# Time mixing reads the previous row from the PSUM bank of the transposed rows

## What is computed

```python
x = x + attention(layernorm(x), Wq, bq, Wk, bk, Wv, bv, Wo, bo)   # softmax(q k^T / 16), causal
h = layernorm(x)
h_prev = rows of h moved down by one, zero in front of each batch
xr = mu_r * h + (1 - mu_r) * h_prev
xk = mu_k * h + (1 - mu_k) * h_prev
x = x + sigmoid(xr @ W_r.T) * (square(relu(xk @ W_k.T)) @ W_v.T)
```

## Time and profile before

| | |
|---|---|
| median of three runs | 363.28 us (363.27 to 363.58) |
| the profiled execution | 363.31 us, span 361.2 us |
| busy, share of the span | PE 98%, DVE 70%, ACT 66%, POOL 58% |
| DVE idle before its maximum (L667), until ACT kept the scores | 47.4 us, 37 times |
| POOL idle before a low part of the weights (L365), until the high part | 37.5 us, 19 times |
| HBM traffic | 10.66 MB, mean 30 GB/s |

### The profile page before, as it was taken

How to read it: one execution, slowest core, us unless ns; L and a number is a source line. 1 busy time by engine, 2 the same in 40 slices (tenths; PEclk the granted TensorE clock), 3 DMA queues, 4 the chain that set the end, 5 groups by cost and what they waited for, 6 DMA issues and landing times.

```text
span 361.2 us, 6799 instructions
## 1 busy us (share of the span) xinstructions
PE 352.3 (98%) x2469; PEld 323.9 (90%) x2469; DVE 253.9 (70%) x571; ACT 239.3 (66%) x468; POOL 208.8 (58%) x246
## 2 busy tenths in 40 slices
PE   8999999999999999999999999999999999999995
PEld 6888888989899898899998989989999999989885
DVE  3696888698946786954568786787767558673645
ACT  2446534988758557696655679577368877789572
POOL 3013230568767753489643257687155768699781
PEclk9999999999999999999999999999999999999999
DMA  7700000000012003003000000120000000000001
GB/s 209 227 2 1 2 0 3 0 3 1 2 48 70 1 2 116 3 0 117 1 3 0 2 0 3 32 86 1 3 29 31 1 2 2 30 31 0 31 29 60
DMA packets 11906, 10.66 MB, mean 30 GB/s; under 512 B 1889, under 2 KB 11874, under 8 KB 11874
## 3 DMA queue, kind: packets, MB, share of 16 engines
q1 hardware_dynamic: 10512, 10.23, 8.7%
q10 hardware_dynamic: 1362, 0.01, 0.2%
HBM read 6.04 MB, written 4.19 MB: 28 GB/s over the span
## 4 chain that ended last, share of the span: by engine, by line
PE 79%; DVE 7%; POOL 6%; ACT 4%; issue 3%; ACTq 0%; DVEq 0%
PE W L801 16%; PE W L798 16%; PE W L802 16%; PE O L971 7%; PE O L973 7%; PE O L972 7%; PE W L834 3%; POOL kT_hi L365 3%; DVE mix L714 2%; POOL mix_lo L370 1%; PE O L996 1%; DVE st L679 1%; ACT mix L472 1%; ACT st L453 1%; DVE h_row L700 1%
## 5 line engine op out<-in xcount | busy, mean ns | idle before, releaser
L365 POOL TENSOR_TENSOR p_lo<-st,p_hi 128x512 fp32r<-128x512 f32 (+1 forms) x71 | 80.9, 1156 | 38.6 <-ACT p_hi L417 37.5
L667 DVE TENSOR_TENSOR peak<-peak,W 128x512 f32<-128x512 f32 (+3 forms) x70 | 42.2, 603 | 47.7 <-ACT st L417 47.4
L417 ACT ACTIVATE st<-W 128x512 f32<-128x512 f32 (+1 forms) x79 | 42.5, 537 | 41.5 <-PE W L802 41.4
L971 PE MATMUL O<-v_hi,p_hi 128*128 128x258 f32 x241 | 69.0, 287 | 0.2 <-DVE x_in L689 0.2
L973 PE MATMUL O<-v_hi,p_lo 128*128 128x258 f32 x241 | 68.0, 282 | 0.0
L972 PE MATMUL O<-v_lo,p_hi 128*128 128x256 f32 x241 | 67.7, 281 | 0.0
L801 PE MATMUL W<-xT_lo,kT_hi 128*128 128x512 f32 (+2 forms) x188 | 65.9, 350 | 0.0
L798 PE MATMUL W<-xT_hi,kT_hi 128*128 128x512 f32 (+2 forms) x188 | 64.3, 342 | 0.0
L802 PE MATMUL W<-xT_hi,kT_lo 128*128 128x512 f32 (+2 forms) x188 | 63.3, 337 | 0.0
L453 ACT ACTIVATE st<-st 128x512 f32<-128x512 f32 (+1 forms) x79 | 44.7, 566 | 8.7 <-DVE st L679 8.6
L370 POOL TENSOR_TENSOR mix_lo<-mix,mix_hi 128x512 fp32r<-128x512 f32 (+2 forms) x36 | 40.4, 1149 | 17.5 <-ACT mix_hi L417 17.5
(11 more groups left out here) (144 smaller groups left out, 825.7 us busy)
## 6 DMA issues: line engine op xcount, KB each, us to landing
out_dram<-gate SPq DMA_DIRECT2D x15, 256.0 KB, 2.2
x_in<-in_L_attn_y_all_dram SPq DMA_DIRECT2D x7, 512.0 KB, 4.4
x_in<-in_L_attn_y_all_dram SPq DMA_DIRECT2D x2, 256.0 KB, 5.1
h_row<-in_L_attn_Wk_dram SPq DMA_DIRECT2D x1, 256.0 KB, 3.6
h_row<-in_L_attn_Wq_dram SPq DMA_DIRECT2D x1, 256.0 KB, 4.5
st<-in_L_attn_Wv_dram SPq DMA_DIRECT2D x1, 256.0 KB, 5.5
st<-in_L_attn_Wo_dram SPq DMA_DIRECT2D x1, 256.0 KB, 5.8
mix<-in_L_ffn_W_k_dram SPq DMA_DIRECT2D x1, 256.0 KB, 6.7
```

Source lines behind the costliest of these rows:

```text
L365: g.tensor_tensor(lo[:, r], score_tile(u), hi[:, r].bitcast(f32), ALU.subtract).then_inc(p_split, 1)
L417: a.activation(dst, src, ACT.Copy, **kw).then_inc(done, 1)
L667: v.tensor_tensor(peak[:, J % 2, r], peak[:, J % 2, r], scores, ALU.max).then_inc(maxed, 1)
L971: mm(o[:, 0:VW], hi[:, r], v_hi[:, j + b, :], start=j + b == 0, stop=False)
```

## The change

The tile hT and its copies go. DVE's mixing reads the row in front from the bank itself, one column to the left, for all columns of the part but the first. The first column's share comes from a small tile `before`: DVE multiplies the last column of each part's bank by (1 - mu) for both kinds, and adds it to the first column of the next part with an operation of its own (none at the start of a batch). The four mixes of a part run by halves of the channels (k and r of half 0, then k and r of half 1), except in the single parts, where the r scales of ACT now come after the high parts of the k mixes. The bank of hT counts as free when both its mixes are done. kk waits for three low parts in place of two (two in a single part). The tables of slots are new throughout; three of them (STATS_AT, APPLY_AT, V_AT) are left out here.

```diff
--- before.py
+++ after.py
@@ -89,6 +89,11 @@
     UNITS = [max(1, n // 2) for G, t0, n in PARTS]
     SINGLE = [K for K, (G, t0, n) in enumerate(PARTS) if n == 1]
 
+    def mix_of(K, i):
+
+
+        return i if K in SINGLE else i % 2 * KC + i // 2
+
     def unit(K, i):
 
         return sum(UNITS[:K]) + i
@@ -111,21 +116,21 @@
 
     FIRST_SLOT = -3
     WARM = (0, 1)
-    PV_AT = [5, 8, 10, 12, 21, 21, 22, 22, 22, 23, 23, 24, 26, 26, 26, 27, 28, 28, 28, 29, 29, 29, 30, 30, 41, 41, 41, 42, 42, 42, 42, 42, 42, 43, 43, 43, 44, 44, 46, 48, 50, 53, 55, 55, 57, 58, 58, 60, 60, 60, 62, 62, 68, 68, 69, 70, 71, 71, 72, 72, 72, 75, 75, 75, 90, 105, 106, 142, 151, 157, 157, 157, 157, 157, 157, 157, 157, 157, 157, 157, 179, 207, 208, 208, 208, 224, 225]
-    MT_AT = [(4,), (17,), (23,), (40,), (44,), (54,), (66,), (72,), (137,)]
-    MB_AT = [(4,), (19,), (23,), (40,), (44,), (54,), (67,), (72,), (147,)]
...
-    XT_AT = {1: (2, 2), 2: (7, 9), 3: (23, 23), 4: (33, 34), 5: (43, 43), 6: (47, 50), 7: (61, 61)}
-    KT_AT = {1: (5, 5), 2: (12, 17), 3: (25, 31), 4: (36, 36), 5: (44, 45), 6: (51, 53), 7: (66, 66)}
...
-    HT_AT = [(19, 22), (27, 28), (33, 35), (51, 52), (58, 58), (69, 69), (112, 115), (193, 197), (197, 207), (248, 268)]
-    MIX_AT = [(22, 22), (28, 28), (35, 38), (52, 52), (58, 58), (69, 72), (136, 136), (199, 205), (213, 226), (287, 352)]
-    KK_AT = [(24, 24), (30, 30), (40, 40), (54, 54), (61, 61), (72, 72), (155, 155), (212, 220), (232, 243), (394, 503)]
-    RR_AT = [(24, 24), (31, 32), (40, 41), (54, 55), (61, 61), (90, 140), (155, 167), (226,), (340,), (509,)]
-    FF_AT = [(27, 27), (33, 33), (41, 42), (57, 57), (67, 68), (112, 137), (179, 205), (358,), (373,), (511,)]
-    END = 512
-    FT_AT = [(-2,), (3,), (3,)]
+    PV_AT = [13, 15, 19, 19, 21, 21, 22, 23, 24, 24, 24, 24, 25, 25, 25, 26, 27, 27, 27, 28, 28, 28, 29, 30, 41, 41, 41, 42, 42, 42, 43, 43, 43, 44, 44, 44, 44, 46, 48, 48, 50, 54, 54, 55, 57, 59, 59, 60, 61, 62, 62, 63, 67, 67, 70, 70, 71, 71, 71, 72, 73, 110, 110, 110, 116, 116, 142, 171, 173, 173, 173, 176, 176, 176, 176, 183, 183, 184, 184, 185, 186, 186, 186, 188, 188, 188, 193]
+    MT_AT = [(9,), (15,), (24,), (40,), (44,), (52,), (64,), (80,), (124,)]
+    MB_AT = [(11,), (17,), (24,), (40,), (45,), (53,), (66,), (98,), (173,)]
...
+    XT_AT = {1: (2, 2), 2: (6, 9), 3: (21, 22), 4: (30, 30), 5: (43, 43), 6: (45, 48), 7: (62, 62)}
+    KT_AT = {1: (5, 5), 2: (12, 16), 3: (24, 29), 4: (32, 36), 5: (45, 46), 6: (51, 55), 7: (63, 67)}
...
+    HT_AT = [(23, 23), (27, 27), (34, 34), (51, 53), (58, 59), (70, 71), (142, 144), (183, 183), (190, 190), (203, 209)]
+    MIX_AT = [(23, 23), (27, 27), (34, 34), (51, 53), (58, 59), (71, 71), (157, 171), (183, 183), (190, 194), (210, 210)]
+    KK_AT = [(25, 25), (29, 29), (39, 39), (55, 55), (61, 61), (79, 98), (174, 174), (187, 188), (196, 197), (212, 438)]
+    RR_AT = [(25, 25), (30, 30), (40, 40), (56, 57), (61, 66), (116, 116), (175, 176), (194,), (197,), (587,)]
+    FF_AT = [(26, 26), (30, 30), (40, 41), (57, 57), (63, 67), (118, 121), (182, 184), (210,), (312,), (1103,)]
+    END = 1104
+    FT_AT = [(-3,), (3,), (7,)]
     IDLE = (6, 1, 3, 0, 0)
 
     def stages(s):
@@ -203,7 +208,8 @@
         p_hi, p_lo = sb("p_hi", [P, NP, GW], f32r), sb("p_lo", [P, NP, GW], f32r)
         peak = sb("peak", [P, 2, GW])
         peak_col = sb("peak_col", [P, 2, TG])
-        hT = sb("hT", [P, KC, GW + 1])
+
+        before = sb("before", [P, 2, 2, KC])
         mix = sb("mix", [P, 2 * KC, GW])
         mix_hi, mix_lo = sb("mix_hi", [P, 2 * KC, GW], f32r), sb("mix_lo", [P, 2 * KC, GW], f32r)
         act = mix[:, 0:KC, :]
@@ -213,7 +219,7 @@
         wvo_hi, wvo_lo = sb("wvo_hi", [P, KC, C], f32r), sb("wvo_lo", [P, KC, C], f32r)
         ffn_hi, ffn_lo = sb("ffn_hi", [P, 3, KC, C], f32r), sb("ffn_lo", [P, 3, KC, C], f32r)
         cols = sb("cols", [P, 7, KC])
-        BQ, BK, BV, MU_R, MU_K, OM_R, OM_K = range(7)
+        BQ, BK, BV, MU_K, MU_R, OM_K, OM_R = range(7)
         first = sb("first", [P, 2, KC])
         minus_first = sb("minus_first", [P, KC])
         ident = sb("ident", [P, P])
@@ -364,9 +370,9 @@
                 hi, lo = weights(u)
                 g.tensor_tensor(lo[:, r], score_tile(u), hi[:, r].bitcast(f32), ALU.subtract).then_inc(p_split, 1)
 
-            def mix_low(J, j):
-                r = span(J)
-                pool.wait_ge(mix_high, 2 * KC * J + j + 1)
+            def mix_low(J, i):
+                j, r = mix_of(J, i), span(J)
+                pool.wait_ge(mix_high, 2 * KC * J + i + 1)
                 g.tensor_tensor(mix_lo[:, j, r], mix[:, j, r], mix_hi[:, j, r].bitcast(f32), ALU.subtract).then_inc(mix_split, 1)
 
             def act_low(J, h):
@@ -458,39 +464,39 @@
                     sc.wait_ge(pv_done, u - NP + 1)
                 high(weights(u)[0][:, cols_of(u)], score_tile(u), p_high)
 
+            def scaled(J, j, mu, h):
+                r = span(J)
+                return a.activation(mix[:, j, r], bank_of("hT", J, h)[:, r], ACT.Copy, scale=cols[:, mu, h:h + 1])
+
             def hT_part(J, h):
-                G, r = PARTS[J][0], span(J)
+                r = span(J)
                 sc.wait_ge(hT_ready, KC * J + h + 1)
                 if J > 0 and h == 0 and r.start == 0:
-                    sc.wait_ge(prev_ready, G + 1)
                     sc.wait_ge(mix_split, 2 * KC * J)
                     sc.wait_ge(act_split, KC * J)
                 if J == 0:
                     sc.wait_ge(ffn_ready, 3)
 
-                def scaled(j, mu, h):
-                    return a.activation(mix[:, j, r], bank_of("hT", J, h)[:, r], ACT.Copy, scale=cols[:, mu, h:h + 1])
-
-                a.activation(hT[:, h, r.start + 1:r.stop + 1], bank_of("hT", J, h)[:, r], ACT.Copy)
                 if J in SINGLE:
 
-                    scaled(h, MU_K, h).then_inc(mu_done, 1)
-                    if h == KC - 1:
-                        for i in range(KC):
-                            scaled(KC + i, MU_R, i).then_inc(mu_r_done, 1)
+                    scaled(J, h, MU_K, h).then_inc(mu_done, 1)
                 else:
-                    scaled(h, MU_K, h)
-                    scaled(KC + h, MU_R, h).then_inc(mu_done, 1)
-
-            def mix_part(J, j):
-                r = span(J)
-                sc.wait_ge(mixed, 2 * KC * J + j + 1)
+                    scaled(J, h, MU_K, h)
+                    scaled(J, KC + h, MU_R, h).then_inc(mu_done, 1)
+
+            def mix_part(J, i):
+                j, r = mix_of(J, i), span(J)
+                sc.wait_ge(mixed, 2 * KC * J + i + 1)
                 if j == 0 and J > 0 and r.start == 0:
                     sc.wait_ge(r_ready, unit(J, 0))
                     sc.wait_ge(ff_ready, unit(J, 0))
                 elif j == 0 and J > 0:
                     sc.wait_ge(k_ready, KC * J)
                 high(mix_hi[:, j, r], mix[:, j, r], mix_high)
+                if J in SINGLE and j == KC - 1:
+
+                    for h in range(KC):
+                        scaled(J, KC + h, MU_R, h).then_inc(mu_r_done, 1)
 
             def kk_part(J, h):
                 n, r = KC * J + h + 1, span(J)
@@ -647,9 +653,8 @@
             dve.wait_ge(fold_moved, 3)
             low(wvo_lo[:], early[0][:].rearrange("p (k c) -> p k c", k=KC), wvo_hi[:], fold_split)
             dve.wait_ge(col_loaded, 48)
-            v.tensor_scalar(cols[:, OM_R:OM_K + 1, :], cols[:, MU_R:MU_K + 1, :], -1.0, 1.0, ALU.mult, ALU.add)\
+            v.tensor_scalar(cols[:, OM_K:OM_R + 1, :], cols[:, MU_K:MU_R + 1, :], -1.0, 1.0, ALU.mult, ALU.add)\
                 .then_inc(om_ready, 1)
-            v.memset(hT[:, :, 0:1], 0.0).then_inc(prev_ready, 1)
 
             def take_max(s):
 
@@ -700,25 +705,29 @@
                 v.tensor_scalar(h_row[:, p, :], x_in[:, G % NX, p, :], mean_var2[:, p, 0:1], rstd2[:, p:p + 1],
                                 ALU.subtract, ALU.mult).then_inc(h_ready, 1)
 
-            def mix_part(J, j):
-                (G, t0, n), r = PARTS[J], span(J)
+            def mix_part(J, i):
+                (G, t0, n), r, j = PARTS[J], span(J), mix_of(J, i)
                 h, om = j % KC, (OM_K, OM_R)[j // KC]
                 if J in SINGLE and j >= KC:
                     dve.wait_ge(mu_r_done, KC * SINGLE.index(J) + h + 1)
                 else:
                     dve.wait_ge(mu_done, KC * J + h + 1)
-                if j == 0:
-                    dve.wait_ge(prev_ready, G + 1)
-                    if J == 0:
-                        dve.wait_ge(om_ready, 1)
-                v.scalar_tensor_tensor(mix[:, j, r], hT[:, h, r], cols[:, om, h:h + 1], mix[:, j, r],
+                if j == 0 and J == 0:
+                    dve.wait_ge(om_ready, 1)
+                bank, c = bank_of("hT", J, h), slice(r.start + 1, r.stop)
+                if G % GB or t0:
+
+                    if j == 0:
+                        dve.wait_ge(prev_ready, KC * J)
+                    if J in SINGLE:
```

(32 more changed lines are left out.)

## The result

| | before | after |
|---|---|---|
| median | 363.28 us (363.27 to 363.58) | 365.36 us (364.1, 365.35, 365.37, 365.77) |
| ratio, 95% interval | | 1.0046 [1.0034, 1.0059] |
| profiled execution, span | 363.31 us, 361.2 us | 364.1 us, 362.3 us |

The change makes the kernel 0.46% slower, 2.1 us. The executions of the changed kernel fall on two levels, about 364.1 and 365.3 us, and the profiled one is of the lower. So its trace can explain only 0.8 of the 2.1 us; the other 1.3 us needed a trace of the upper level (first experiment).

A forecast was written before the change was run, and what follows sets the result against it. PE, busy 98%, was taken to bound the kernel, so only its waits count. Terms +1.45 - 1.2 + 0 + 1.7, less 0.25 for overlap, gave +1.7 on 363.28: 365.0 us, range 362.3 to 367.0.

The forecast's parts named there:

- group 2's banks: Near 138 us, S(36) and kT(4,1) wait for banks that hT holds longer: +1.45 us, bounds 0.8 to 2.6.
- 77 and 95 us: PE's waits before mt(2), 1.05 us, and at an O bank, 0.36 us, go under the new tables.
- S(21), and the start: DVE has more work than PE in slots 17 to 20: S(21) waits 0.4 us; the start's waits change by -0.2.
- POOL's queue, 310 to 338: ff(6,0) waits some 1.6 us behind POOL's low parts, where similar waits stand now: 0, from -1 to +1.
- tail: Last two one-tile parts: new waits at kk(8,0), kk(9,0) and kk(9,1), less waits removed: +1.7 us, bounds +0.3 and +3.
- overlap: Taken off the sum because the waits overlap, a late PE finding later queues further on: 0.25 us.
- Part 1: Engine work: ACT some 10 us lighter, DVE 3 lighter to 10 heavier, mixes steady at 0.68 us; mostly off PE's path.
- Part 2: Banks of hT stay held until mixed, 3.7 us after hT's start; PE waits at group 2: +1.45 us.
- Part 3: New tables early on: gaps at 77 and 95 us go, S(21) waits 0.4: -1.2 us, from -1.6 to +0.3.
- Part 4: POOL's queue from the last mb on: ff(6,0) waits some 1.6 us; term 0, from -1 to +1.
- Part 5: The tail: kk(8,0) waits 1.2 us, kk(9,0) about 1.5 including ff(7,0), kk(9,1) 0.3; net +1.7.
- held small additions: Rival: POOL holds DVE's new additions up to 1.1 us, about two hits: 366.8 us; chance 0.18, shared with a larger tail.

The follow-up runs named there:

- first experiment: The changed kernel run once more without any edit, its profiled execution on the upper level: 365.27 us, ratio 1.0043 to the kernel before.
- the exchange: The changed kernel with all four mixes of part 8 in slot 190, ahead of the last tile's x1_part: 365.88 us, ratio 1.0069 to the kernel before.

## Why the prediction came out as it did

365.0 was forecast, 365.36 measured, and slower by over 0.2% was the likeliest sign. But that the number is so near is luck, by errors of opposite signs: the visible waits come to less than the sum had them, and an event that it didn't have makes up for it.

| step | forecast, us | measured, us |
|---|---|---|
| group 2's banks | +1.45 | +0.69 + 0.52 = +1.2 |
| 77 and 95 us | -1.05 - 0.36 | -1.05 - 0.36 |
| S(21), and the start | +0.4 - 0.2 | 0, and within 0.1 |
| 228 us | 0 | +0.32 |
| POOL's queue, 310 to 338 | 0 | 1.35 + 0.33 - 0.89 - 0.42 - 0.28 = +0.1 |
| tail | +1.7 | 0.78 + 0.41 + 0.59 - 0.43 - 0.63 = +0.7 |
| overlap | -0.25 | |
| sum of the visible | +1.7 | +0.9 (span +1.1, time +0.8) |
| h_row held, upper level | not there | +1.2 |

- Part 1. The mixes with a PSUM input are steady, as forecast; their records are 0.74 us, not 0.68, and they save 3.7 us on the 28 large ones, not 5 to 6. ACT gets 6.1 us lighter, not some 10. Small operations were priced at 0.17 us each. Their records are that long (0.15 to 0.16, below), but the next instruction starts 0.07 after them, so on a path they cost 0.07 where POOL is idle. The sentence that work taken off ACT "is worth nothing by itself" was drawn from the kernel before, whose PE never waited in the middle; no run tests it there. On the changed kernel it is wrong: putting the copies back costs 4.8 us, which the new tables have already spent.
- Part 2. The mechanism was right and shown at S(36): 0.52 us with the new mixing, none with the old one in the same slots, 1.00 with the copies back. Size: the bank is free 3.53 us after hT's start (136.46 to 139.99, the end of the second mix), forecast 3.7; the two small operations were mis-sized by 0.1 each. DVE in the changed kernel:

```profile
138.45 0.16 DVE L725 TENSOR_TENSOR mix<-mix,before 128x2 f32<-128x2 f32 x1 [0.47 <-ACT mix L469]
138.52 0.74 DVE L729 SCALAR_TENSOR_TENSOR mix<-W,cols,mix 128x511 f32<-128x511 f32 x1
139.19 0.15 DVE L727 TENSOR_TENSOR before<-cols,W 128x2 f32<-128x2 f32 x1
139.25 0.74 DVE L729 SCALAR_TENSOR_TENSOR mix<-W,cols,mix 128x511 f32<-128x511 f32 x1
```

  But the larger part, 0.69 at S(35), is another step, which I didn't have: S(35) takes the bank of S(34), and its maximum (137.29 to 137.98) can't start before ACT has kept the scores. This wait comes from the tables; it is the same with the old mixing. I had put all on S(36) and kT(4,1); what PE waits at S(35) it need not wait at S(36), and so the term, 1.2 for 1.45, still came out near.
- Part 3. Both gaps went as forecast. The DVE overload that was to cost S(21) 0.4 us doesn't show.
- Part 4. The wait at ff(6,0) was forecast at 1.6 and is 1.35, and the term 0 holds at +0.1. The run with POOL's two subtractions moved shows the cause.
- Part 5 was mis-sized. kk(8,0) waits 0.78, not 1.2; ff(7,0) and kk(9,0) together 1.00, not 1.26 (1.5 less the keep-warm matmul that falls in); kk(9,1) not at all, forecast 0.3. The x1 part's share at kk(8,0) is shown by the exchange (0.33). kk(9,0) waits, as forecast, for the second k low, which ends at 354.18, 0.10 before PE starts (the row names the mix ahead of it). That the mixing and not the order makes these waits is not shown: with the old mixing in the new tables they are nearly as long. I had again charged 0.17 for each small operation and taken every step of each chain one after the other.
- What failed outright is the list of places: none of its steps asks what an instruction that the change leaves as it is will meet at its new time. The held h_row is the mechanism of the rival "held small additions" in another instruction, and with its price (1.1 us). The additions themselves are held too (one took 1.35 us at 337), but together they cost 0.4 us.
- Of the signs named beforehand, the missing gap before mt(2) came. The wait for a mix near 138 us was 0.52 and not 1.4, those before kk(8,0) and kk(9,0) stayed under 1 us, and the mixing takes 0.74. New gaps between 100 and 300 us, the sign of dear small operations, came too (0.32 at 228, 1.05 at 211), but both stay without the additions (0.30 and 1.06): the sign pointed at the wrong cause.

What stays open: which executions fall on which level; the 0.1 to 0.2 us by which the held case costs more than its 1.05 us wait; and how much of the loss the new mixing makes and how much the new order, outside group 2. Taking h_row out of POOL's way without other moves wasn't found.

## What to carry to other kernels

A copy that decouples two engines can be dead weight on its own engine and still be what frees a bank early: before it is dropped, compare for each user of the rotation the new hold time with the work that lies before that bank's next use. A gain in engine time off the path is worth what the next order of the work makes of it, so ask for both kernels what their orders have spent. And where two engines can hold each other up, as DVE and POOL do here, an order of work puts unchanged instructions at new moments: look for any that start while the other engine is in a run of back-to-back instructions and that have a waiting engine behind them.

## What the runs showed of the hardware

- A 128x256 operation of DVE that arrives 1.13 to 1.14 us into the first of POOL's two 1.26 us subtractions took 0.41 us in one execution and 1.54 in another of the same program, and the executions are 1.2 us apart (364.1 and 365.3). Their starts before it differ by 0.05 us; what decides isn't shown.
- The additions on 128x2 elements took from 0.15 to 1.35 us with the same work: held, a tiny operation is as dear as a large one (1.25 in the run with pv 40 later, behind an h_row of 1.28). The 18 multiplications of the same size that read the bank in PSUM took 0.14 to 0.15 us every time.
- A DVE operation on two columns is recorded as 0.15 to 0.16 us, and the next starts 0.07 after it: durations of small instructions overstate their cost in a queue.
- After 4 us without work PE was granted a clock of 0.50 for 5 us, and lost 2.3 us more by it.
